# Flamingo layer: row sums inside the mixing product, two mixing banks, two projection banks, another order of each step

## What is computed

```python
# x, ctx: (16, 128, 1024); 8 heads of 16 channels, window of 16 positions
def xattn(x, cond):                       # x is layernormed over the last axis
    q, k, v = Wq @ x + bq, Wk @ cond + bk, Wv @ cond + bv
    k, v = pad(k, 8, 7), pad(v, 8, 7)
    dots = sum_d q[h, d, t] * k[h, d, t + w] * scale          # w in 0..15
    out = sum_w softmax(dots)[h, t, w] * v[h, d, t + w]
    return Wo @ out + bo
def ffn(x):                               # int4-like weights, groups of 128
    gate, up, down = (dequantize(w, s, z) for each)
    return (silu(x @ gate) * (x @ up)) @ down
x = x + tanh(g_xattn) * xattn(layernorm(x), ctx)
x = x + tanh(g_ffn) * ffn(layernorm(x))
```

## Time and profile before

| | us |
|---|---|
| median of 3 runs | 1725.99 |
| lowest and highest of them | 1715.70, 1726.87 |
| the profiled execution | 1736.66 |
| its span in the trace | 1734.8 |
| PE busy | 1607.8 (93%) |
| DVE busy | 1516.9 (87%) |
| POOL busy | 1455.0 (84%) |
| ACT busy | 995.8 (57%) |

### The profile page before, as it was taken

The page is one execution under the profiler, slowest core; times in us unless marked ns, Lnnn a source line. Parts: engine busy times, 40 slices in busy tenths (PEclk is TensorE's granted clock), DMA queues, the critical chain, the costliest instruction groups (busy, mean ns, idle before and its releaser), DMA issues.

```text
span 1734.8 us, 40469 instructions
## 1 busy us (share of the span) xinstructions
PE 1607.8 (93%) x16614; PEld 823.8 (47%) x16614; DVE 1516.9 (87%) x1482; ACT 995.8 (57%) x1134; POOL 1455.0 (84%) x892
## 2 busy tenths in 40 slices
PE   6888889889658999999999999999999999999996
PEld 4565656566533444444444444444444444444444
DVE  4567667667539999999999999999999999999996
ACT  3566667666534555555555555555555555555552
POOL 4556646565647999999999999999999999999975
PEclk8899989899869999999999999999999999999998
DMA  5645645565333222222222222222222222222127
GB/s 120 154 110 150 140 120 132 128 137 126 96 97 97 74 74 73 73 79 79 75 73 73 75 81 76 73 73 73 74 80 78 73 74 74 78 78 76 37 97 291
DMA packets 162354, 166.66 MB, mean 96 GB/s; under 512 B 11918, under 2 KB 127310, under 8 KB 162154
## 3 DMA queue, kind: packets, MB, share of 16 engines
q1 hardware_dynamic: 161018, 163.74, 33.7%
q10 hardware_dynamic: 1152, 0.33, 0.1%
HBM read 113.92 MB, written 16.78 MB: 75 GB/s over the span
## 4 chain that ended last, share of the span: by engine, by line
PE 81%; issue 6%; POOL 5%; ACT 3%; DMA 1%; DVE 1%; SPq 1%; ACTq 0%; POOLq 0%; DVEq 0%
PE bank L1136 63%; PE bank L1043 3%; POOL oacc L564 3%; PE bank L1032 2%; PE bank L999 2%; PE bank L1075 2%; PE bank L1006 2%; PE bank L991 2%; ACT pT L632 2%; PE bank L1053 1%; ACT xn L639 1%; PE bank L1022 1%; PE bank L995 1%; PE bank L1003 1%; PE bank L1011 1%
## 5 line engine op out<-in xcount | busy, mean ns | idle before, releaser
L924 DVE SCALAR_TENSOR_TENSOR acc<-bank,scale,acc 128x1024 f32<-128x1024 f32 x784 | 949.3, 1271 | 17.7 <-PE bank L1136 10.3
L1136 PE MATMUL bank<-xT,w_int 128*128 128x512 f16 x3584 | 851.3, 381 | 12.0 <-ACT acc L733 4.3
L564 POOL TENSOR_TENSOR oacc<-oacc,d_part 128x1024 f32<-128x1024 f32 x336 | 795.0, 2366 | 26.5 <-ACT d_part L753 10.3
L753 ACT ACTIVATE d_part<-bank,scale 128x1024 f32<-128x1024 f32 x336 | 373.5, 1112 | 390.7 <-PE bank L1136 376.8
L1136 PEld LDWEIGHTS bank<-xT,w_int 128*128 128x128 f16 x3584 | 350.5, 98 | 439.4 <-DVE acc L924 7.1
L1136 PE MATMUL bank<-h_hi,d_int 128*128 128x512 f16 x896 | 340.2, 380 | 7.2 <-ACT d_part L753 3.0
L1136 PE MATMUL bank<-h_lo,d_int 128*128 128x512 f16 x896 | 339.5, 379 | 0.0
L506 POOL TENSOR_TENSOR raw_z<-raw_w,raw_z 128x512 int32<-128x512 int32 x168 | 263.9, 1571 | 29.0 <-DMA raw_z<-in_L_ffn_gate_z_dram 12.2
L632 ACT ACTIVATE pT<-bank 96x1024 f16<-96x1024 f16 x128 | 123.4, 1014 | 61.2 <-PE bank L1043 61.2
L1136 PEld LDWEIGHTS bank<-h_hi,d_int 128*128 128x128 f16 x896 | 87.2, 97 | 150.1 <-DVE acc L924 27.8
L820 DVE TENSOR_REDUCE rmax<-bank 128x16 f32<-128x768 f32 x64 | 60.9, 952 | 104.6 <-PE bank L1032 104.6
(11 more groups left out here) (82 smaller groups left out, 1406.1 us busy)
## 6 DMA issues: line engine op xcount, KB each, us to landing
raw_w<-in_L_ffn_gate_w_dram SPq DMA_DIRECT2D x56, 256.0 KB, 3.0
raw_z<-in_L_ffn_gate_z_dram SPq DMA_DIRECT2D x56, 256.0 KB, 3.7
raw_w<-in_L_ffn_up_w_dram SPq DMA_DIRECT2D x56, 256.0 KB, 3.0
raw_z<-in_L_ffn_up_z_dram SPq DMA_DIRECT2D x56, 256.0 KB, 3.7
raw_w<-in_L_ffn_down_w_dram SPq DMA_DIRECT2D x56, 256.0 KB, 2.7
raw_z<-in_L_ffn_down_z_dram SPq DMA_DIRECT2D x56, 256.0 KB, 3.3
vt<-vn_hl SPq DMA_DIRECT2D x64, 192.0 KB
vt<-vn_hl SPq DMA_DIRECT2D x64, 160.0 KB
```

The source lines that it names most:

```text
L564: nc.gpsimd.tensor_tensor(into, into, part, ALU.add).then_inc(d_added, 1)
L753: nc.scalar.activation(d_part[:, (count(0, x, False) - 1) % 2, :], pair[slot][:, :, :].rearrange("p h r -> p (h r)"), ACT.Copy, scale=scal ...
L924: nc.vector.scalar_tensor_tensor(out=into, in0=pair[u % 4][:, :, :].rearrange("p h r -> p (h r)"), scalar=scale[:, par, i, m, k:k + 1], in ...
L1136: last = nc.tensor.matmul(dst[:, h, :], weights, rows_of(h, part), start=(part == 0), stop=(part == 1))
```

## The change

1. v gets 33 columns per head in place of 32: 16 high, 16 low and a one (`V1`). The product with v so gives the sum in its 33rd column. `add_up`, the column of ones and DVE's separate `invert_sums` are gone; `take_mix` takes the reciprocal from the 33rd columns. POOL writes the ones once, before v is moved for the first time.
2. 16 heads' results at 33 columns do not fit into one bank: `mix` writes banks 6 and 7, in strips of 64 columns. The ring of projection banks shrinks from three to two.
3. PE's order in a step: scores, first and second task, mixing, third task, turning.
4. DVE empties the third task in its own step, behind the second, and takes the mixed values between the first and the second.
5. ACT takes second and third task before the turned probabilities; `norm_x` moves from the end of s = 0 to its front.
6. POOL normalizes step n - 2 behind `split_p(n)`, in place of n - 3 ahead of it.

```diff
+    V1 = 2 * HD + 1
+    VS = 64
-        vn_hl = sb("vn_hl", [P, NV, HEADS, 2, HD], fp16, att)
+        vn_hl = sb("vn_hl", [P, NV, HEADS, V1], fp16, att)
...
-        proj, score, mixed = (bank[0], bank[1], bank[7]), bank[2:4], bank[6]
+        proj, score, mixed = bank[0:2], bank[2:4], bank[6:8]
...
-        all_mixed = mixed[:, 0:JG * HEADS * 2 * HD].rearrange("p (x a d) -> p x a d", a=2, d=HD)
+        all_mixed = pair[3][:, :, :].rearrange("p g (h e) -> p (g h) e", e=VS)
...
+            sp.wait_ge(ones_placed, 2)
             place_v(0)
...
             nc.gpsimd.tensor_copy(ident16[:, :], ident[:, :]).then_inc(masks_made, 1)
+            nc.gpsimd.memset(vn_hl[:, :, :, 2 * HD], 1.0).then_inc(ones_placed, 1)
+            nc.gpsimd.memset(v_pad[:, :, 2 * HD], 1.0).then_inc(ones_placed, 1)
...
-                    if S * b + s >= 3:
-                        normalize(S * b + s - 3)
...
                     split_p(b, s)
+                    if S * b + s >= 2:
+                        normalize(S * b + s - 2)
...
-                    behind_scores, behind_mix, behind_turn = tasks_of(b, s)
-                    for t in behind_scores:
+                    if s == 0 and b + 1 < B:
+                        norm_x(b + 1)
+                    first, second, third = tasks_of(b, s)
+                    for t in first:
                         take_high(*t)
                     exp(n)
-                    for t in behind_mix:
+                    for t in second + third:
                         take_high(*t)
                     if n:
                         take_pT(n - 1)
-                    for t in behind_turn:
-                        take_high(*t)
-                    if s == 0 and b + 1 < B:
-                        norm_x(b + 1)
...
-                if n >= 3:
-                    invert_sums(n - 3)
                 dve.wait_ge(max_ready, n + 1)
...
-            def invert_sums(n):
-                dve.wait_ge(sums_ready, n + 1)
-                if n >= 2:
-                    dve.wait_ge(normalized, n - 1)
-                nc.vector.reciprocal(rinv[:, n % 2], sums_at(n)).then_inc(sums_inverted, 1)
...
-                nc.vector.tensor_reduce(o_sum[:, n % 2], all_mixed.rearrange("p x a d -> p x d a"), AX.X, ALU.add)\
-                    .then_inc(mix_taken, 1)
+                nc.vector.reciprocal(rinv[:, n % 2], all_mixed[:, :, 2 * HD]).then_inc(sums_inverted, 1)
+                nc.vector.tensor_reduce(o_sum[:, n % 2], all_mixed[:, :, 0:2 * HD].rearrange("p x (a d) -> p x d a", a=2),
+                                        AX.X, ALU.add).then_inc(mix_taken, 1)
...
                     soften(b, s)
-                    if n:
-                        for t in tasks_of((n - 1) // S, (n - 1) % S)[2]:
-                            take_low(*t)
-                    for t in tasks_of(b, s)[0]:
+                    first, second, third = tasks_of(b, s)
+                    for t in first:
                         take_low(*t)
                     if n >= 2:
                         take_mix(n - 2)
-                    for t in tasks_of(b, s)[1]:
+                    for t in second + third:
                         take_low(*t)
...
-            dve.wait_ge(sums_ready, S * B - 1)
-            invert_sums(S * B - 3)
-            invert_sums(S * B - 2)
-            for t in tasks_of(B - 1, S - 1)[2]:
-                take_low(*t)
             take_mix(S * B - 2)
...
-                            last = nc.tensor.matmul(
-                                mixed[c, to:to + 2 * HD], pT[0:2 * KW, n % 2, h // HG, at:at + QB],
-                                vt[b % 2][0:2 * KW, slot_of(JQ * s + JJ * jg + jj), h].rearrange("p a d -> p (a d)"),
-                                start=True, stop=True)
+                            last = nc.tensor.matmul(mixed[jg][c, VS * h:VS * h + V1], pT[0:2 * KW, n % 2, h // HG, at:at + QB],
+                                                    vt[b % 2][0:2 * KW, slot_of(JQ * s + JJ * jg + jj), h, :],
+                                                    start=True, stop=True)
...
-                    if n >= 3:
-                        add_up(n - 3)
                     scores(b, s)
-                    behind_scores, behind_mix, behind_turn = tasks_of(b, s)
-                    for t in behind_scores:
+                    first, second, third = tasks_of(b, s)
+                    for t in first + second:
                         project(*t)
                     if n >= 2:
                         mix(n - 2)
-                    for t in behind_mix:
+                    for t in third:
                         project(*t)
                     if n == 1:
                         pe.wait_ge(s_kept, 2)
                     if n:
                         turn_probs(n - 1)
-                    for t in behind_turn:
-                        project(*t)
-            pe.wait_ge(shifted, S * B)
-            add_up(S * B - 3)
-            add_up(S * B - 2)
             mix(S * B - 2)
```

More of the change, by code:

```diff
@@ L86, in flamingo_layer @@
         km = [sb("km0", [P, 2, HG, T + WIN], fp16, att)]
-        vt = [sb("vt0", [P, NJ, HEADS, 2, HD], fp16, att)]
+        vt = [sb("vt0", [P, NJ, HEADS, V1], fp16, att)]
         q_hl.append(sb("q_hl1", [P, 2, T], fp16, att))
         km.append(sb("km1", [P, 2, HG, T + WIN], fp16, att))
-        vt.append(sb("vt1", [P, NJ, HEADS, 2, HD], fp16, att))
+        vt.append(sb("vt1", [P, NJ, HEADS, V1], fp16, att))
         rows.append(sb("row1", [P, T], fp32, att))
@@ L127, in flamingo_layer @@
         bv_all = xr[:, 0:C]
-        v_pad = xr[:, C:2 * C].bitcast(fp16).rearrange("p (h a d) -> p h a d", a=2, d=HD)
+        v_pad = xr[:, C:C + HEADS * V1 // 2].bitcast(fp16).rearrange("p (h e) -> p h e", e=V1)
         V_MOVES = 16 * 2 * (VW + 2)
@@ L139, in slot_of @@
             return j % VW * NV + j // VW
-        def sums_at(n):
-            at = JQ * KW + JG * HEADS * (n % 2)
-            return bank[4][:, 0:JG * HEADS] if n == S * B - 1 else score[0][:, at:at + JG * HEADS]
         att.close()
@@ L172, in flamingo_layer @@
         bias_turned, bias_summed, bias_ready = sem("bias_turned"), sem("bias_summed"), sem("bias_ready")
[L173 removed]
+        pad_hi, pad_lo, pad_placed, ones_placed = sem("pad_hi"), sem("pad_lo"), sem("pad_placed"), sem("ones_placed")
         x_loaded = [sem("even_x_loaded"), sem("odd_x_loaded")]
@@ L185, in flamingo_layer @@
         probs_turned, pT_ready, mix_ready = sem("probs_turned"), sem("pT_ready"), sem("mix_ready")
-        sums_ready, sums_inverted, mix_taken, normalized, turned_back = (
-            sem("sums_ready"), sem("sums_inverted"), sem("mix_taken"), sem("normalized"), sem("turned_back"))
+        sums_inverted, mix_taken, normalized, turned_back = (
+            sem("sums_inverted"), sem("mix_taken"), sem("normalized"), sem("turned_back"))
         s_loaded, s_turned, s_kept = sem("s_loaded"), sem("s_turned"), sem("s_kept")
@@ L609, in take_high @@
                         act.wait_ge(v_placed, V_MOVES * b)
-                    nc.scalar.activation(vn_hl[:, 4 * n:4 * n + 4, :, 0, :],
+                    nc.scalar.activation(vn_hl[:, 4 * n:4 * n + 4, :, 0:HD],
                                          src.rearrange("p (n h d) -> p n h d", h=HEADS, d=HD), ACT.Copy)\
@@ L678, in _ @@
             act.wait_ge(bv_loaded, 16)
-            nc.scalar.activation(v_pad[:, :, 0, :], bv_all.rearrange("p (h d) -> p h d", d=HD), ACT.Copy, scale=-1.0)\
+            nc.scalar.activation(v_pad[:, :, 0:HD], bv_all.rearrange("p (h d) -> p h d", d=HD), ACT.Copy, scale=-1.0)\
                 .then_inc(pad_hi, 1)
@@ L684, in _ @@
             act.wait_ge(bias_turned, 1)
-            nc.scalar.activation(bo_sum[:, :], mixed[:, 0:1], ACT.Identity, bias=bias[:, 2:3]).then_inc(bias_summed, 1)
+            nc.scalar.activation(bo_sum[:, :], mixed[0][:, 0:1], ACT.Identity, bias=bias[:, 2:3]).then_inc(bias_summed, 1)
             act.wait_ge(bias_summed, 1)
@@ L857, in take_low @@
                 if kind == "v":
-                    hi, lo = (vn_hl[:, 4 * n:4 * n + 4, :, part, :] for part in range(2))
+                    hi, lo = (vn_hl[:, 4 * n:4 * n + 4, :, HD * part:HD * part + HD] for part in range(2))
                     nc.vector.tensor_tensor(lo, src.rearrange("p (n h d) -> p n h d", h=HEADS, d=HD), hi,
@@ L880, in _ @@
             dve.wait_ge(pad_hi, 1)
-            nc.vector.scalar_tensor_tensor(out=v_pad[:, :, 1, :], in0=bv_all.rearrange("p (h d) -> p h d", d=HD),
-                                           scalar=-1.0, in1=v_pad[:, :, 0, :],
+            nc.vector.scalar_tensor_tensor(out=v_pad[:, :, HD:2 * HD], in0=bv_all.rearrange("p (h d) -> p h d", d=HD),
+                                           scalar=-1.0, in1=v_pad[:, :, 0:HD],
                                            op0=ALU.mult, op1=ALU.subtract).then_inc(pad_lo, 1)
@@ L1044, in turn_probs @@
                 last.then_inc(probs_turned, 1)
-            def add_up(n):
```

(15 more changed lines are left out.)

8 lines of the change are left out of this document (1 added, 7 removed).

## The result

The changed kernel takes 1700.05 us (median of 4 runs, 1697.10 to 1702.19) against 1725.11 before in the same comparison: a ratio of 0.9864, 95% interval 0.9825 to 0.9904, so 25 us less. The forecast was 12 us less (1714). The result lies inside the stated range of 1690 to 1744, but under the 1703 to 1737 of the forecast's own case, and 4 us above the 1696 of rival B.

What follows compares the result with a forecast made beforehand. PE, nearest to full though no engine is full, was taken to bound the attention stage; -4 (twelve batches), -5 (batches 0 to 3) and -6 (end) made -15, less 3 given back: -12, 1714 us. Range 1690 to 1744.

Steps and rivals of the forecast that it cites:

- the forecast's own case: Whole kernel: the summed gains in the attention stage and its end, 12 us less, 1714 us; chance 0.46.
- rival B: Attention batches: idle places on PE swallow nearly all issue waits and low-clock stretches; batch 26.1 us, -30, 1696; chance 0.30.
- What bounds: Attention stage and the seam behind it, 445.7 us: every term comes from there; PE nearest to full, no engine full.
- The quiet batch, 24.3 to 25.3: Attention batch without disturbance: sums and old wait won, 2.7 us; about 3.7 us lost to bank waits, partly behind `norm_x`.
- Batches 0 to 3, -5: First four attention batches: each wins 1.64 + 1.1 less about 1.2 of ring waits; -5 us (0 to -9).
- The end, -6: End of attention: o1 emptied directly behind o0, so POOL's wait for the fourth weight piece ends sooner; -6 us (-3 to -8).
- The mixing at 33 columns, the ones: Mixing products and POOL's memsets: wider products taken as nothing (+0 to +6 us), ones hidden behind loads (0 to +0.5).
- Rival D: Mixing in attention: the 33-column products take twice as long; +5 us on the forecast, 1719; chance 0.06.
- The other 12 batches, 27.7 to 27.4, -4: Later attention batches: quiet 25.3 plus 2.1 us of surplus against 27.7, times 12; -4 us (-23 to +12).
- I take them to 0.6, and the remaining 1.8 to 1.5: Surplus above a quiet batch, 3.4 us: mixing issue waits from 1.6 to 0.6, other waits and low clock 1.8 to 1.5.
- I give back 3 us because more idle on PE will leave the clock low a little more often: PE clock in attention: 3 us of the summed gain lost to low clock, -15 becoming -12.
- Rival C: Attention clock: idle ahead of k1 drops PE to 1.2 GHz in s = 1; 2.7 us a batch, 1746; chance 0.18.

Runs made afterwards that it cites:

- `normx_behind_k1`: Changed kernel with `norm_x` moved in ACT's list from the front of s = 0 to behind k1's high half: 1679.62 us, ratio 0.9719.
- `before_again`: The kernel before, unchanged, run once more for a second trace: 1724.64 us.
- `seam_alone`: Kernel before with only o1 of the last step projected ahead of the turning and emptied ahead of the last sums: 1722.76 us, ratio 0.9973.
- the long run: The first profiled execution of the unchanged kernel before: 1736.66 us, 10.7 us above the median of its runs.
- `both_norms_moved`: Changed kernel with `norm_x` behind k1's high half and `norm_row` behind q0's, ahead of exp: 1670.88 us, ratio 0.9664.
- `parts12_old_order`: Changed kernel with the order of before on PE, ACT and DVE, POOL as in the change: 1726.82 us, ratio 1.0005.
- `sums_kept_unread`: Changed kernel with PE still making the 16 one-column products of the sums per step, read by nobody: 1699.14 us, ratio 0.9834.
- The order alone: Kernel before with only the new lists of PE, ACT and DVE, keeping the sums and three banks: 1683.27 us, ratio 0.9728.

## Why the prediction was right and where it was short

- *What bounds*: right. All of the difference lies in the attention stage and at its end.
- *The quiet batch, 24.3 to 25.3*: right, 25.22, step by step within 0.1 us, with `norm_x`, x_end and k1 as the longest link. That this link is the cause, and not only present, `normx_behind_k1` shows: 20 us for one moved call.
- *Batches 0 to 3, -5*: they went from 107.0 us (`before_again`, 24.6 to 131.6) to 100.9 (25.4 to 126.3), -6. The terms as written, 1.64 + 1.1 - 1.2 in each of four batches, make -6 and not -5.
- *The end, -6*: -6.1 as counted above; `seam_alone` has it at -7.6 (1284.9 against 1292.5).
- *The mixing at 33 columns, the ones*: nothing, as taken. Rival D is out.
- *The other 12 batches, 27.7 to 27.4, -4*: this is the term that was mis-sized. Batches 4 to 14 take 26.06 us each ((413.0 - 126.3) / 11) against 27.24 in `before_again`, and 0.84 above the quiet batch, where I had left 2.1. That is -13 over eleven batches (-22 against the 28.05 of the long run, on which the forecast rested). The step that failed is "I take them to 0.6, and the remaining 1.8 to 1.5": the waits in the mixing did go to 0.66 a batch (10.6 / 16), but those in scores and sums went too, from 5.5 us (13 in the long run) to 1.1, so that the whole surplus fell to 0.84. The clock has no visible part in the -13, since it is 0.94 in both traces.
- *"I give back 3 us because more idle on PE will leave the clock low a little more often"*: not borne out. The granted clock over the stage is 0.94, as in `before_again` and above the 0.90 of the long run, though PE idles for 73 us and not 66. Rival C is out. The rule of the Trainium skill (TensorE: Matmul & The Clock Gate, "A second HAM failure mode: psum-queue depth-cycling") would have made it the likely one, and the traces here do not agree with it: `both_norms_moved` too has short bank waits in most steps, and a granted clock of 0.98 from 25 to 390 us.
- Rival B's outcome came: 12 us of issue waits, 26.06 us a batch where B had 26.1. Its reason, that idle PE lets instructions arrive, holds in part. The new order goes with fewer issue waits even without idle places for banks, 26 and 22 us in the two kernels with three banks against 33 to 43 in the old order (24 where v was not moved); with the idle places of two banks they are 12 to 15, in all five kernels of that kind. Idle places in the old order did not do it: 34 us in `parts12_old_order`, with 37 us of them. The other reason that B named, fewer instructions, has no part in it (`sums_kept_unread`).
- *The chances*: the prediction gave 0.36 to a gain of more than 17 us and 0.46 to a time within 17 us of before; the less likely of the two came. The stated range took the result in because it reached down to B, not because the forecast's own sum was near: of that sum the chain and the end came as worked out, and the surplus, 9 us more, and the 3 us given back came otherwise. Both errors go the same way.
- Not seen at all: that the change pulls in two directions. The order alone is worth 43 us, and the rest of the change takes 17 of them back, because the ring of two ties k1 to x_end, and x_end stands behind `norm_x`. I had written down both halves of this and not asked what the order would do with three banks.

The Trainium skill (Runtime: NRT & Kernel Launch, "Instruction fetch mechanics") has it that crossing a block of instructions is mostly hidden. By count the traces agree, for in before 61 of 80 loads of instructions are followed by no issue wait. By price they don't: the other 19 cost 38 us of the stage, and the rule led to no gain at all from hidden waits, where the measured one is 25 us with 21 us of issue waits fewer.

## What to carry to other kernels

Where engines work lists in order and share a short ring of banks, follow one bank from its release back through every list; a call that waits in front of a list can be dear (here `norm_x`, 1.24 us of work a batch, cost 20 us in all), and its best place here lay between the last user that must not wait and the first that needs it. Count a quiet period first and the surplus over it apart: an edit that shortens the one can lengthen the other (8 us won for a wait of 16 to 18). When a change has several parts, price them crosswise; here the part in its name (the sums) was worth nothing, and the order alone more than the whole (43 us against 25).
